# A chunked recurrence with sixteen history units a leaf: the units spread over all sixteen steps in the orders of PE and ACT

## What is computed

```python
def step(St, inp):
    kt, qt, vt, at, bt = inp
    Sk = jnp.einsum('bhij,bhj->bhi', St, kt)
    err = Sk - vt
    Sn = at[..., None] * St - (bt[..., None] * err)[..., None] * kt[:, :, None, :]
    ot = jnp.einsum('bhij,bhj->bhi', Sn, qt)
    return (Sn, ot)
```

## Time and profile before

| what | us |
|---|---|
| median of 3 runs | 3042.21 |
| lowest and highest of them | 3035.08, 3061.76 |
| the profiled execution | 3051.64 |
| its span, first to last instruction | 3050.0 |
| start of leaf 0 of the recurrence on DVE | 681.6 |
| start of leaf 1, the first with units | 743.7 |
| end of leaf 14, the last with units | 1861.0 |

### The profile page before, as it was taken

How to read it: one execution, slowest core, us unless ns; L and a number is a source line. 1 busy time by engine, 2 the same in 40 slices (tenths; PEclk the granted TensorE clock), 3 DMA queues, 4 the chain that set the end, 5 groups by cost and what they waited for, 6 DMA issues and landing times. The chain is left out here.

```text
span 3050.0 us, 41308 instructions
## 1 busy us (share of the span) xinstructions
PE 2080.3 (68%) x12114; PEld 1426.5 (47%) x12114; DVE 1852.3 (61%) x4462; ACT 1056.3 (35%) x2356; POOL 1183.0 (39%) x1443
## 2 busy tenths in 40 slices
PE   8999999966766666556556446599967553479700
PEld 4555555534555554444345335578733331157600
DVE  5777777767776677776667548545537482023234
ACT  2555555534444444444334234222300100112200
POOL 1444444446443333333333323244444217311175
PEclk8999999987787787787777777799989565579955
DMA  3666666663677788999999993422221602048732
GB/s 93 121 121 121 120 121 121 121 148 71 155 189 176 198 210 222 232 243 240 245 241 251 263 281 82 155 76 76 77 83 33 218 11 71 1 144 264 219 101 84
DMA packets 680751, 457.64 MB, mean 150 GB/s; under 512 B 309583, under 2 KB 625790, under 8 KB 674312
## 3 DMA queue, kind: packets, MB, share of 16 engines
q1 hardware_dynamic: 550891, 314.96, 40.9%
q0 software_dynamic: 50080, 96.70, 11.8%
q10 hardware_dynamic: 79616, 44.06, 5.0%
HBM read 245.54 MB, written 207.77 MB: 149 GB/s over the span
## 5 line engine op out<-in xcount | busy, mean ns | idle before, releaser
L918 ACT ACTIVATE p_diag_o<-p_ident,p_gd 128x128 f32<-128x128 f32 x1152 | 361.7, 389 | 509.2 <-PE p_ps_o L874 483.2
L384 DVE SCALAR_TENSOR_TENSOR p_y<-p_ps_proj,p_w,p_y 128x508 f32<-128x508 f32 (+2 forms) x576 | 416.0, 741 | 115.4 <-ACT p_y L298 101.8
L874 PE MATMUL p_ps_o<-p_ws,p_diag_o 128*128 128x128 f32 x1792 | 327.3, 340 | 128.4 <-DVE p_ws L620 80.0
L726 POOL DMA_DIRECT2D p_near_g<-gram x512 | 284.5, 565 | 289.3 <-PE p_ps_n L847 288.8
L874 PEld LDWEIGHTS p_ps_o<-p_ws,p_diag_o 128*128 128x128 f32 x1792 | 284.0, 240 | 200.6 <-DVE p_ws L620 101.8
L833 PE MATMUL p_ps_z<-p_turned,p_gcol 112*32 112x128 f32 x3584 | 159.6, 319 | 318.3 <-DMA p_turned<-history 318.2
L234 PE MATMUL p_ps_proj<-p_x,p_w 128*128 128x512 f32 x768 | 343.1, 597 | 2.7 <-ACT p_beta_t L289 2.7
L198 POOL TENSOR_TENSOR p_kq<-p_y,p_sig 128x512 f32<-128x512 f32 x128 | 162.2, 1271 | 377.6 <-ACT p_sig L309 376.9
L833 PEld LDWEIGHTS p_ps_z<-p_turned,p_gcol 112*32 112x32 f32 x3584 | 104.7, 126 | 382.4 <-DMA p_turned<-history 343.0
L570 DVE SCALAR_TENSOR_TENSOR p_zo<-p_ws,p_gd,p_zo 128x128 f32<-128x128 f32 x768 | 243.9, 351 | 3.8
L564 DVE TENSOR_TENSOR p_ws<-p_ws,p_dec 128x128 f32<-128x128 f32 (+2 forms) x192 | 119.0, 620 | 205.7 <-PE p_ps_o L874 205.7
(11 more groups left out here) (223 smaller groups left out, 3837.0 us busy)
## 6 DMA issues: line engine op xcount, KB each, us to landing
history<-p_hist SPq DMA_DIRECT2D x18, 2048.0 KB, 14.9
gram<-p_gram SPq DMA_DIRECT2D x64, 512.0 KB, 5.4
history_sums<-p_sums ACTq DMA_DIRECT2D x112, 256.0 KB, 5.5
p_zo<-history_sums SPq DMA_DIRECT2D x28, 1024.0 KB, 8.3
p_wgu<-in_wguT SPq DMA_DIRECT2D x64, 352.0 KB
decays<-p_dec SPq DMA_DIRECT2D x64, 256.0 KB, 2.3
beta_v<-p_bv SPq DMA_DIRECT2D x64, 256.0 KB, 2.5
p_dec<-decays POOLq DMA_DIRECT2D x32, 512.0 KB, 6.5
```

The costliest lines, as they stand in the source:

```text
L384: nc.vector.scalar_tensor_tensor(out=yv[:, :, s:], in0=pv[:, :, 0:T - s], scalar=par[j % 2][:, kind, TAPS - 1 - s:TAPS - s], in1=yv[:, :, ...
L726: pool.dma_start(near_g[h * HALF:(h + 1) * HALF, :, f, h, :], gram_dram[g * BG:(g + 1) * BG, c, c * C:c * C + HALF, h, e0:e0 + HALF] .rear ...
L874: nc.tensor.matmul(ps_o[s // 4 % 2][:, s % 4, :], diag_o[p // DO % NDO][:, p % DO, :], rows[:, r, :], start=(s % 4 == 0 and r == 0), stop= ...
L918: last = nc.scalar.activation(diag_o[n % NDO][:, p % DO, :], ident[:], ACT.Copy, scale=gd[g][:, r, s:s + 1])
```

## The change

The table gets sixteen entries, one for each step of a leaf, and both engines' loops run over all sixteen steps, with the near work at the middle.

```diff
-    UNITS_AFTER = (0, 0, 1, 2, 2, 2, 3, 3)
-    UNITS_NEAR = UNITS - sum(UNITS_AFTER)
+    UNITS_AFTER = (0, 0, 0, 0, 1, 1, 2, 4, 2, 1, 1, 1, 1, 1, 1, 0)
+    assert sum(UNITS_AFTER) == UNITS
...
-                for s in range(HALF):
+                for s in range(C):
+                    if s == HALF:
+                        pe.wait_ge(near_g_in, (at + 1) * 2 * H * DMA)
+                        near_product(at, 0)
+                        near_turn(at, 0)
+                        near_product(at, 1)
+                        near_turn(at, 1)
                     own_rows(at, s)
                     while u < min(units, sum(UNITS_AFTER[:s + 1])):
                         history(at - 1, u)
                         u += 1
-                pe.wait_ge(near_g_in, (at + 1) * 2 * H * DMA)
-                near_product(at, 0)
-                near_turn(at, 0)
-                near_product(at, 1)
-                while u < units:
-                    history(at - 1, u)
-                    u += 1
-                near_turn(at, 1)
-                for s in range(HALF, C):
-                    own_rows(at, s)
...
-                for s in range(HALF):
+                for s in range(C):
+                    if s == HALF:
+                        near_rows(at, 0)
+                        near_rows(at, 1)
                     made = past(s, made)
                     while (b + 1) * UB <= min(units, sum(UNITS_AFTER[:s + 1])):
                         batch_row(at - 1, b)
                         b += 1
-                near_rows(at, 0)
-                near_rows(at, 1)
-                while b * UB < units:
-                    batch_row(at - 1, b)
-                    b += 1
-                for s in range(HALF, C):
-                    made = past(s, made)
```

## The result

The changed kernel takes 3101.68 us (median of 4 runs, 3098.65 to 3103.82). The kernel before has 3038.64 beside it (4 runs, 3034.59 to 3061.76). The ratio is 1.0191, with a 95% interval of [1.0138, 1.0244]: slower by about 2%. The two profiled executions lie 49.1 us apart, 3100.77 with a span of 3099.1 against 3051.64 with 3050.0; what follows adds up on that scale.

A forecast was written before the change was run, and what follows sets the result against it. It took a loop as the bound: SP's second `zo` load, its store-and-load chain, the next leaf's sixteen history units, and that load again. Leaf periods gave +47 us, relief -14, so +33: 3075 us from 3042.21, range 3025 to 3125.

The forecast's parts named there:

- The loop z-to-u0, u0-to-v, v-to-z: A leaf's period is the sum of these three stretches; the change puts DVE's second half inside it: +47 us together.
- z-to-u0: SP's second `zo` load issue (z) to the next leaf's first history unit (u0): kept at 28.1 to 43.9 us, c=2 to 6.
- u0-to-v: First history unit to end of step 8 (v): 24.3 us, 25.8 from history chunk c=4 (leaves 9 and 10) on.
- v-to-z: End of step 8 to SP's issue of the second `zo` load, behind the last batch's sums: 27.0 us.
- DVE would start each leaf 11 us late: At each leaf's start from leaf 2 on, DVE waits about 11 us for the sums of the leaf before.
- L564 would nearly vanish: DVE's waits for `ps_o` behind history units, 194.1 us in 42 places before, nearly disappear.
- Such a reload takes about 7 us: Reloading a freed buffer with a later unit's history rows takes about 7 us, in both halves of a leaf.
- The relief: POOL's `dec[1]` and `near_g` loads no longer fall into SP's history store: 1.2 us in 12 leaves, -14 us.
- Leaves 1 and 2 at 70.6: Without stored history the leaf start counts: step 8 ends at 36.0, then 27.0 and 7.6 us, pair +7.7.
- Much slower: Rival, chance 0.12: reloads in the second half come late and delay the last batch, +92 us, 3134.
- No change: Rival, chance 0.37: z-to-u0 shortens by 3 us in 12 leaves rather than 1.2, +11 us, 3053.
- Faster: Rival, chance 0.13: z-to-u0 shrinks further, by at least 6.5 us a leaf; at 7.5 us 2999.

The follow-up runs named there:

- Three late: Kernel before with only its last three history units moved from between the near products to behind steps 12 to 14: 3210.25 us against 3042.88, ratio 1.0559.
- front 8: Changed kernel with its eight second-half units packed forward, three behind step 8, three behind step 10, two behind step 12: 3096.11 us, ratio 1.0188.
- First 13: Kernel before with no unit in the first four steps, thirteen still ahead of the near products, three in the near work: 2955.97 us against 2980.35, 0.9909.

## Why the prediction was right, and where it was off

Direction and mechanism were right, the size too small: +33 us were forecast and +49.1 came between the profiled executions (+63 between the medians). That the sum came as near as it did is in part luck: one step was 56 us too small, and three others together 37 too large. By its steps:

- *The loop z-to-u0, u0-to-v, v-to-z* holds. Three late pays nearly all of it: that kernel was forecast by it at 3214 and took 3210.
- *DVE would start each leaf 11 us late*: 141.5 in 13 places is 10.9. *L564 would nearly vanish*: 194.1 to 24.4.
- *u0-to-v is 24.3, or 25.8 for c from 4.* This is the step that failed. It was 24.9 at c=1 and then 28.9, 30.5, 29.9, 32.0 and 32.2 for c=2 to 6. Twice the differences is 1.2 + 9.2 + 12.4 + 8.2 + 12.4 + 12.8 = 56.2 us too little. Inside it, "Such a reload takes about 7 us" is what broke. From u0 to u4, where 12 us were taken by ACT's and PE's work alone, it was 15.4 on the mean of leaves 5 to 14, with u4 waiting for its rows; from u4 to u7 8.7 for 7 (16.9 and 7.2 in leaf 10, below). From u7 to v it was 6.6 for 5.3, and here the granted clock counts: leaf 2 took 5.3 us at 1.00 (2.4 GHz) and leaf 12, with the same products, 7.6 at 0.50 (1.2 GHz). From u0 to u7, ahead of it, PE had been busy for 10.3 of 14.9 us in leaf 2 and for 13.4 of 24.5 in leaf 12. I had read the 7 us of a reload where POOL sent nothing beside it, and checked the 18.8 of u0 to u7 where `near_w` came only in the last 6 us. That step 7 ends 19.6 us after the start was right, and I did not follow it to POOL, which waits for step 7.
- *v-to-z is 27.0.* It was 24.2, 23.7, 24.4, 25.0, 27.1 and 27.7 for c=1 to 6, which is 19.8 us less over both leaves. The last sums landed in 2.2 to 3.3 us in leaves 1 to 11, where 4.6 had been taken, and in 4.4 to 4.6 in leaves 12 to 14, where v to z was 25.8 to 29.6. DVE needed 17.3 rather than 18.0 at best, and 18.0 on the mean of leaves 5 to 14.
- *The relief.* z-to-u0 was 21.9, 24.6, 29.6, 34.4, 38.3 and 40.3 for c=1 to 6; against the forecast less 1.2 that is another 6 us less. Right in kind and about the size.
- *Leaves 1 and 2 at 70.6.* They took 65.0, since v came at 32.5 and not at 36, and z 23.8 behind it and not 27: 11 us less. 7 us for a reload was too much there, where a unit has 16 rows and u4 to u7 took 4.

33 + 56 - 20 - 6 - 11 = 52, against 52.9 measured for these leaves. The windows u7 to v of leaves 2 and 12, with the granted clock as the third number from the end:

```profile
837.70:843.00 5.30, 4.62 (x40) 4.43 (x40) 2.81 (x5) 2.25 (x4) 0.00 (x0) 1.00 0.71 209
1670.10:1677.70 7.60, 6.92 (x31) 6.63 (x32) 1.77 (x4) 1.75 (x3) 0.00 (x0) 0.50 0.58 154
```

*The rivals.* Much slower took reloads in the second half to be late; they were, in front 8, but in the changed kernel DVE took 17.3 us from v to step 14 in most leaves up to leaf 9, and 17.3 to 19.8 from there on. The lateness was real and stood mainly in the first half. No change rested on z-to-u0 being 3 us shorter in 12 leaves; leaf by leaf against before it was 2.2 (33.6 to 31.5 on the mean), and that rival had no cost in u0-to-v. Faster fell with z-to-u0, which would have had to shrink by 6.5 us and shrank by 3.5, 0.5, -0.6, 0.8 and 3.6 for c=2 to 6 against the earlier trace rows.

The reason why the first half grew can be seen in POOL's program. In leaf 10 before, then in the changed kernel (timeline: start us, us, engine, line):

```profile
1442.62 4.20 POOL L716 DMA_DIRECT2D p_near_w<-p_w  x8 [9.23 <-DVEq L633]
```

```profile
1453.71 1.08 PE L833 MATMUL p_ps_z<-p_turned,p_gcol 112*32 112x128 f32 x16 [13.07 <-DMA p_turned<-history]
...
1457.67 1.08 PE L833 MATMUL p_ps_z<-p_turned,p_gcol 112*32 112x128 f32 x16
...
1458.41 4.20 POOL L716 DMA_DIRECT2D p_near_w<-p_w  x8
...
1462.54 0.63 POOL L693 DMA_DIRECT2D p_dec<-decays  x1
...
1470.62 1.08 PE L833 MATMUL p_ps_z<-p_turned,p_gcol 112*32 112x128 f32 x16 [5.57 <-DMA p_turned<-history]
...
1475.50 3.36 PE L833 MATMUL p_ps_z<-p_turned,p_gcol 112*32 112x128 f32 x48 [3.80 <-DMA p_turned<-history]
```

Before, `near_w` left 13 us after u0 ended (1429.52). Now it leaves 3.6 us after it (1454.79), with `dec[0]` 4.1 us behind, both into the reloads. The buffer of u4 is free when u1 ends, at 1458.75, and that of u5 when u2 ends, near 1461.7; u4 starts 11.9 us after the first and u5 13.8 after the second, at 1475.50. The DMA issues from the end of u0 to v, before (1429.52 to 1468) and after (1454.8 to 1485), with KB each and the median us from issue to landing:

```profile
history_sums<-p_sums ACTq DMA_DIRECT2D x6, 256.0 KB, 5.7
...
p_near_w<-p_w POOLq DMA_DIRECT2D x8, 64.0 KB, 2.8
p_dec<-decays POOLq DMA_DIRECT2D x1, 512.0 KB, 7.0
```

```profile
history_sums<-p_sums ACTq DMA_DIRECT2D x4, 256.0 KB, 8.6
...
p_near_w<-p_w POOLq DMA_DIRECT2D x8, 64.0 KB, 8.0
p_dec<-decays POOLq DMA_DIRECT2D x1, 512.0 KB, 13.0
```

Everything in the shared stretch lands later, the small copies most of all. It is so in every leaf from 5 on: 7.0 to 8.5 us for a `near_w` copy (2.4 to 4.7 before), 11.2 to 14.0 for `dec[0]` (5.7 to 9.6). In leaves 1 to 4, which lost nothing, `near_w` leaves 6.6 to 8.8 us behind u0 and lands in 2.6 to 4.8. Over leaves 5 to 14 the change took 8.1 us out of u0 to v (eight units in it instead of thirteen) and put 15.6 into v to z. First 13 has the later u0 of the change but no units in the second half, and is faster than before.

## What to carry to other kernels

Before moving work later, look for the loop that crosses queues: what does the last of it release, and does that start the next iteration's chain? Here the last batch's DMA gates SP's whole program for the next leaf, so what it moves back is paid once a leaf (three late: z 13.9 us later behind v, 12.6 us a leaf), with the queues at 82 GB/s meanwhile. It does not follow that moving it forward wins the same: packed units (front 8) won nothing. And when an engine is sped up past a point, list who waits for that point: here step 7 sends POOL's copies, and they met the very loads that the plan rested on.

## What the runs showed of the hardware

- DMAs of several queues that run side by side stretch each other unevenly. In leaf 10 of the changed kernel, where all of them stood in one stretch of 237 GB/s, a 64 KB `near_w` copy took 8.0 us for 2.8 before, a 512 KB `dec` load 13.0 for 7.0, and a 1 MB store 8.9 for 8.1.
- The last sums of a leaf (256 KB) landed in 2.2 to 3.3 us in leaves 1 to 11 of the changed kernel, while the queues carried 118 to 149 GB/s, and in 4.4 to 4.6 in leaves 12 to 14, at 212 to 227. The list of DMA issues from 1505 to 1511, in leaf 10:

```profile
history_sums<-p_sums ACTq DMA_DIRECT2D x1, 256.0 KB, 2.2
```

- For the near products and turns ahead of v, PE was busy 4.6 us at a granted clock of 1.00 and 6.9 at 0.50 (leaves 2 and 12 of the changed kernel).

The Trainium skill's fit ("DMA: Bandwidth & Descriptors", "Anatomy of one DMA — SWDGE (gpsimd) path"), written for another path, has 2.6 us for the 256 KB as an estimate. I had set it aside for the 4.6 of a loaded leaf; here the trace comes near it. For the 1 MB `zo` load the estimate is 4.4, and the trace has 7.6 at best and 9.6 here, so there it doesn't hold.
